# Mamba scan between two expert layers: decays two chunks ahead, two banks for the scan's outputs

## What is computed

```python
def _mamba2(u, Wi, conv_w, conv_b, dt_bias, A_log, D, norm_w, Wo):
    zxbcdt = u @ Wi.T                                    # z, xBC, dt
    xBC = silu(causal_conv4(xBC) + conv_b)               # x, B, C
    dt, A = softplus(dt + dt_bias), -exp(A_log)
    h = h * exp(dt_t * A) + (dt_t * x_t) B_t             # token by token
    y_t = h C_t + D * x_t
    y = y * silu(z)
    y = y * rsqrt(mean(y * y) + 1e-05) * norm_w
    return y @ Wo.T
x = x + 0.5 * moe(layernorm(x))
x = x + (out_f + out_b[:, ::-1]) * 0.5
x = x + 0.5 * moe(layernorm(x))
```

## Time and profile before

| what | us |
|---|---|
| median of 3 runs | 824.81 (816.74 to 825.22) |
| the profiled execution | 823.38 |
| its span in the trace | 821.5 |
| granted clock of PE, mean | 0.955 of full speed |

### The profile page before, as it was taken

One profiled execution on the slowest core, in us unless ns is written; L12 is line 12 of the kernel. 1 busy time (PEld: TensorE's weight loads), 2 busy tenths in 40 slices (PEclk: granted clock), 3 DMA queues, 4 the chain that ended last, 5 costly groups with the idle time before them and its releaser, 6 DMA issues. The chain is left out here.

```text
span 821.5 us, 13087 instructions
## 1 busy us (share of the span) xinstructions
PE 719.1 (88%) x4076; PEld 382.0 (46%) x4076; DVE 491.8 (60%) x1424; ACT 544.1 (66%) x936; POOL 278.3 (34%) x296
## 2 busy tenths in 40 slices
PE   4799999989999997898988976798897787999996
PEld 1432222212123224565655554667675675566564
DVE  6878542204865647852456659779698776533453
ACT  4367998899998993653357675884988552434441
POOL 3090003301000433434522455242443470255552
PEclk9899999999999998999989998798999899999999
DMA  4046925522492311111211032121221231222233
GB/s 135 1 180 180 191 78 95 206 75 70 175 285 79 100 38 43 35 41 52 67 55 55 20 113 66 40 64 49 73 62 40 83 96 35 65 60 58 64 100 92
DMA packets 76409, 70.10 MB, mean 85 GB/s; under 512 B 9687, under 2 KB 60233, under 8 KB 76080
## 3 DMA queue, kind: packets, MB, share of 16 engines
q1 hardware_dynamic: 71024, 60.56, 26.4%
q0 software_dynamic: 5024, 8.54, 3.2%
q10 hardware_dynamic: 288, 0.10, 0.1%
HBM read 41.23 MB, written 29.02 MB: 86 GB/s over the span
## 5 line engine op out<-in xcount | busy, mean ns | idle before, releaser
L693 ACT ACTIVATE attn_p<-attn_ps 128x1024 f32<-128x1024 f32 x256 | 241.0, 1079 | 26.0 <-PE attn_ps L686 14.6
L709 PE MATMUL attn_ps<-attn_p,attn_v 128*32 128x512 f32 x1024 | 136.4, 604 | 5.7 <-issue 5.6
L1687 PE MATMUL ps_main<-moe_xsT,moe_w 128*128 128x320 f32 x384 | 128.2, 460 | 9.1 <-issue 3.1
L1697 ACT ACTIVATE moe_act_h<-ps_main 128x320 f32<-128x320 f32 (+1 forms) x128 | 55.3, 434 | 98.3 <-PE ps_main L1687 67.4
L1712 DVE TENSOR_TENSOR moe_hid<-moe_act_h,ps_main 128x320 f32<-128x320 f32 (+1 forms) x128 | 62.0, 485 | 96.1 <-ACT moe_act_h L1697 58.0
L1580 POOL DMA_INDIRECT moe_slots<-rows,moe_scatter_at x64 | 63.6, 994 | 104.6 <-DVE moe_hid L1712 56.0
L1687 PEld LDWEIGHTS ps_main<-moe_xsT,moe_w 128*128 128x128 f32 x384 | 69.1, 196 | 42.8 <-issue 21.2
L686 PE MATMUL attn_ps<-attn_q_rows,attn_k_rows 64*128 64x512 bf16 x448 | 79.8, 385 | 6.3 <-issue 3.0
L1717 PE MATMUL ps_main<-moe_hid,moe_w 128*128 128x320 f32 (+1 forms) x256 | 75.5, 461 | 4.6 <-DVE moe_hid L1712 4.6
L686 PEld LDWEIGHTS attn_ps<-attn_q_rows,attn_k_rows 64*128 64x128 bf16 x448 | 19.0, 93 | 122.2 <-ACT attn_p L693 96.6
L2119 DVE SCALAR_TENSOR_TENSOR mb_act<-mb_padded,mb_taps,mb_act 128x1024 f32<-128x1024 f32 x48 | 67.1, 1408 | 1.3 <-ACT mb_act L2110 0.7
(11 more groups left out here) (268 smaller groups left out, 1304.3 us busy)
## 6 DMA issues: line engine op xcount, KB each, us to landing
mb_cums<-mb_cum_kept SPq DMA_DIRECT2D x32, 256.0 KB, 3.5
moe_slots<-zeros SPq DMA_DIRECT2D x4, 1380.0 KB, 13.4
attn_q_rows<-attn_q_parts SPq DMA_DIRECT2D x36, 128.0 KB
attn_k_rows<-attn_k_parts SPq DMA_DIRECT2D x36, 128.0 KB
moe_w<-in_w SPq DMA_DIRECT2D x3, 1536.0 KB, 11.3
moe_rows<-zeros SPq DMA_DIRECT2D x4, 1024.0 KB, 14.7
...
```

The source lines that it names most:

```text
L693: self.core.nc.scalar.activation(self.p[:, w % self.PB, :, :].rearrange("p a n -> p (a n)"), self.ps_s[:, w % self.SB, :, :].rearrange("p ...
L709: ins = self.core.nc.tensor.matmul(self.ps_av[32 * i:32 * i + 32, :], self.v[:, b * TPB + kt, (HGROUPS * i + m) // 2, self.window(m)], sel ...
L1687: self.core.nc.tensor.matmul(ps[:, w % 2, 0:CAP], wt[:, e, c * P:(c + 1) * P], self.xsT[:, u % 2, :], start=True, stop=True).then_inc(self ...
L1697: self.core.nc.scalar.activation(self.act_h[into, w % 2, :], self.ps_h1[rows, w % 2, 0:CAP], ACT.Silu).then_inc(self.silu_done, 1)
```

## The change

ScalarE's work for a chunk is split in three: `lower` (the four Relus), `copy_b` and `exps`. Before the loop it does lower, copy and exponential of chunk 0 and lower and exponential of chunk 1; in iteration `g` it begins with `lower(g+2)`, `copy_b(g+1)`, `exps(g+2)`. `cums` and `e_seg` get a third place, in columns of `moe.hid`, which is why SP waits for the last expert's `y_done` before the sums of chunk 2. SP's loop runs one longer, and the spread decays are issued two behind the sums.

`ps_y` has two banks and `ps_x` one. PE does `outputs(g)` right after `state(g)`, then `squares` and `output`, then the projections. The sums of squares of the last four chunks go to spare columns of `ps_st`; those of chunks 28 to 31 are formed after the loop, the last behind the last `output`.

The norm's roots move to chunk 6, its normalise for tiles 18 and 19 to chunk 6 (20 and 21 from chunk 5 to 6 of unit 2); turn, logits, routing and counts of the last expert layer each one chunk later; scatters from chunks 1 to 6 of unit 3 (3, 3, 3, 3, 3, 1) to chunks 2 to 6 (3, 3, 3, 3, 4). After the scan DVE takes the first expert's rows before the last adds, and the root search and normalise of the last tiles come between the first gatings, with turns and logits later to match. The cut diff leaves out lines that only rename a buffer's place, and lines around; its indentation is reduced.

```diff
@@ -1885,8 +1885,8 @@
-self.ps_b, self.ps_y, self.ps_st, self.ps_o = (main[:, i, :] for i in (1, 3, 4, 5))
-self.ps_x = (main[:, 0, :], main[:, 2, :])
+self.ps_x, self.ps_b, self.ps_st, self.ps_o = (main[:, i, :] for i in (0, 1, 4, 5))
+self.ps_y = (main[:, 3, :], main[:, 2, :])
@@ -1992,9 +1992,11 @@
-if g >= 2:
-    sp.wait_ge(self.lowered, g - 1)
-sp.dma_start(self.cums[:, g % 2, :, :], self.cum_dram[b, di, j].unsqueeze(0).to_broadcast([P, NH, P])).then_inc(self.cums_in[g % 2], 16)
+if g == 2:
+    sp.wait_ge(self.core.moe.y_done, B * E_)
+if g >= 3:
+    sp.wait_ge(self.lowered, g - 2)
+sp.dma_start(self.cums[g % 3], self.cum_dram[b, di, j].unsqueeze(0).to_broadcast([P, NH, P])).then_inc(self.cums_in[g % 3], 16)
@@ -2132,11 +2134,11 @@
-act, ps_x = self.act_t[:, u % 2, :, :], self.ps_x[g % 2]
+act, ps_x = self.act_t[:, u % 2, :, :], self.ps_x
...
-if g >= 2:
-    pe.wait_ge(self.x_read, g - 1)
-    pe.wait_ge(self.gm_done, g - 1)
+if g >= 1:
+    pe.wait_ge(self.x_read, g)
+    pe.wait_ge(self.gm_done, g)
@@ -2147,23 +2149,27 @@
-def exps(self, act, g):
+def lower(self, act, g):
...
-    act.wait_ge(self.cums_in[g % 2], 16 * (g // 2 + 1))
+    act.wait_ge(self.cums_in[g % 3], 16 * (g // 3 + 1))
...
-    if g >= 2:
-        act.wait_ge(self.mt_done, g - 1)
+    if g >= 3:
+        act.wait_ge(self.mt_done, g - 2)
...
-        ins = nc.scalar.activation(self.e_seg[:, g % 2, hh, :], self.cums[:, g % 2, hh, :], ACT.Relu, bias=self.cum[:, di, n, hh:hh + 1], scale=-1.0)
+        ins = nc.scalar.activation(self.e_seg[g % 3][:, hh, :], self.cums[g % 3][:, hh, :], ACT.Relu, bias=self.cum[:, di, n, hh:hh + 1], scale=-1.0)
...
+def copy_b(self, act, g):
...
-    nc.scalar.copy(self.bs[:, g % 2, :], self.ps_b[:, 0:P]).then_inc(self.b_read, 1)
+    self.core.nc.scalar.copy(self.bs[:, g % 2, :], self.ps_b[:, 0:P]).then_inc(self.b_read, 1)
...
+def exps(self, act, g):
...
-    nc.scalar.activation(self.e_seg[:, g % 2, :, :], self.e_seg[:, g % 2, :, :], ACT.Exp, scale=-1.0).then_inc(self.seg_exp, 1)
+    self.core.nc.scalar.activation(self.e_seg[g % 3], self.e_seg[g % 3], ACT.Exp, scale=-1.0).then_inc(self.seg_exp, 1)
@@ -2240,19 +2246,20 @@
-if g >= 1:
-    pe.wait_ge(self.y_read, g)
+ps_y = self.ps_y[g % 2]
+if g >= 2:
+    pe.wait_ge(self.y_read, g - 1)
@@ -2292,23 +2299,26 @@
-    if parts:
+    if u == 3 and i >= GROUP:
+        pe.wait_ge(self.h_ready, len(self.UNITS) * (self.NC - 1))
+    elif parts:
...
-    if u == 3 and i == GROUP:
-        pe.wait_ge(self.ss_read, 4)
-    col = 3 * D + n % TPB
+    at = self.sums_of(u)[:, n % TPB:n % TPB + 1] if u < 3 or i < GROUP else self.sums_of(4)[:, i:i + 1]
...
-        ins = self.core.nc.tensor.matmul(self.ps_o[:, col:col + 1], self.y2[:, g % 3, c, :], self.ones[:, 0:1], start=(c == 0), stop=(c == 1))
+        ins = self.core.nc.tensor.matmul(at, self.y2[:, g % 3, c, :], self.ones[:, 0:1], start=(c == 0), stop=(c == 1))
...
+def sums_of(self, k):
+    return self.ps_st[:, DIN:DIN + TPB] if k == 4 else self.ps_o[:, 3 * D:3 * D + TPB]
...
-    self.core.nc.vector.tensor_scalar(self.var[:, lo:hi], self.ps_o[:, 3 * D + lo:3 * D + hi], 1.0 / DIN, None, ALU.mult).then_inc(self.ss_read, 1)
+    self.core.nc.vector.tensor_scalar(self.var[:, lo:hi], self.sums_of(k)[:, lo:hi], 1.0 / DIN, None, ALU.mult).then_inc(self.ss_read, 1)
@@ -2326,7 +2336,8 @@
-pe.wait_ge(self.ss_read, self.scale_of(u, part) + 1)
+if self.scale_of(u, part) < 4:
+    pe.wait_ge(self.ss_read, self.scale_of(u, part) + 1)
@@ -2369,6 +2380,7 @@
+mamba.e_seg, mamba.cums = ([own[:, 0, :, :], own[:, 1, :, :], moe.hid[:, 1, :, i * P:(i + 1) * P]] for i, own in enumerate((mamba.e_seg, mamba.cums)))
@@ -2449,21 +2461,19 @@
-if u == 1 and i == 0:
-    pe.wait_ge(norm.ready, 20)
-if u + 1 < UNITS and i != mamba.GATES_AT:
-    for c in mamba.PIECES_AT[i]:
-        mamba.project(pe, u + 1, c)
+mamba.outputs(pe, g)
...
-if g >= 2:
+if 2 <= g <= N - 3:
...
-mamba.outputs(pe, g)
...
-if u + 1 < UNITS and i == mamba.GATES_AT:
-    mamba.project(pe, u + 1, 5)
+if u == 1 and i == 0:
+    pe.wait_ge(norm.ready, 20)
+if u + 1 < UNITS:
+    for c in mamba.PIECES_AT[i]:
+        mamba.project(pe, u + 1, c)
@@ -2471,23 +2481,24 @@
-    if u == 2 and i == 6:
+    if u == 2 and i == 7:
...
-    if u == 2 and i == 7:
+    if u == 3 and i == 0:
...
-    if u == 3 and i == 0:
+    if u == 3 and i == 1:
...
+for g in range(N - 4, N - 1):
+    mamba.squares(pe, g, 0)
+mamba.output(pe, UNITS - 1, 2)
+mamba.squares(pe, N - 1, 0)
...
-for g in (N - 2, N - 1):
-    mamba.squares(pe, g, PARTS_OUT * (UNITS - 1) + 2)
-mamba.output(pe, UNITS - 1, 2)
@@ -2509,9 +2520,11 @@
-if u == HALF and c in (1, 2):
-    norm.turn(pe, 21 + c)
-if u == HALF and c == 3:
+if u == HALF and c == 0:
+    pe.wait_ge(mamba.ss_read, len(mamba.SCALES))
+if u == HALF and c in (2, 3):
+    norm.turn(pe, 20 + c)
+if u == HALF + 1 and c == 0:
@@ -2537,13 +2550,13 @@
-for g in range(2, N + 1):
+for g in range(2, N + 2):
...
-    if g >= 3:
-        mamba.spread_decays(sp, g - 1)
+    if g >= 4:
+        mamba.spread_decays(sp, g - 2)
@@ -2576,8 +2589,8 @@
-if u == 3 and i >= 1:
-    moe.scatter(pool, 3, 3 * (i - 1), min(3 * i, TOPK * TPB))
+if u == 3 and 2 <= i <= 6:
+    moe.scatter(pool, 3, 3 * (i - 2), 3 * (i - 1) + (i == 6))
@@ -2671,8 +2684,9 @@
-if u == 0 and i in (5, 6):
-    norm.normalise(dve, ch, i + 13)
+if u == 0 and i == 6:
+    norm.normalise(dve, ch, 18)
+    norm.normalise(dve, ch, 19)
@@ -2681,20 +2695,19 @@
-    if u == 2 and i == 5:
+    if u == 2 and i == 6:
...
-    if u == 2 and i == 7:
+    if u == 3 and i == 0:
...
-    if u == 3 and i == 0:
+    if u == 3 and i == 1:
...
+moe.take(dve, HALF)
...
-moe.take(dve, HALF)
...
-norm.invert(dve, ch, 22)
@@ -2707,8 +2720,11 @@
-if u == HALF and c in (0, 1):
-    norm.normalise(dve, ch, 22 + c)
+if u == HALF and c == 0:
+    norm.invert(dve, ch, 22)
+if u == HALF and c == 1:
+    norm.normalise(dve, ch, 22)
+    norm.normalise(dve, ch, 23)
@@ -2771,13 +2787,27 @@
+mamba.lower(act, 0)
+mamba.copy_b(act, 0)
...
+mamba.lower(act, 1)
+mamba.exps(act, 1)
...
+    if g + 2 < N:
+        mamba.lower(act, g + 2)
...
-        mamba.exps(act, g + 1)
+        mamba.copy_b(act, g + 1)
+    if g + 2 < N:
+        mamba.exps(act, g + 2)
...
+    if u == 0 and i == mamba.GATES_AT:
+        norm.root(act, 18)
+        norm.root(act, 19)
+    if u == 2 and i == mamba.GATES_AT:
+        norm.root(act, 20)
+        norm.root(act, 21)
@@ -2795,9 +2825,6 @@
-if u == 0 and i == 5:
-    norm.root(act, 18)
-    norm.root(act, 19)
@@ -2805,13 +2832,10 @@
-if u == 2 and i == 5:
-    norm.root(act, 20)
-    norm.root(act, 21)
-if u == 2 and i == 6:
+if u == 2 and i == 7:
...
-if u == 2 and i == 7:
+if u == 3 and i == 0:
```

More of the change, by code:

```diff
@@ L1897, in open @@
         self.lowered = sem("lowered")
-        self.cums_in, self.e_cum_in = ([sem(f"{n}{i}") for i in range(2)] for n in ("cums_in", "e_cum_in"))
+        self.cums_in, self.e_cum_in = [sem(f"cums_in{i}") for i in range(3)], [sem(f"e_cum_in{i}") for i in range(2)]
         (self.gm_done, self.mt_done, self.xw_done, self.h_decayed, self.h_ready, self.y_read, self.gate_done) = (
@@ L2182, in front @@
                 dve.wait_ge(self.xw_done, self.passed(g - 2))
-        ps_x = self.ps_x[g % 2]
+        ps_x = self.ps_x
         nc.vector.tensor_tensor(self.by_head(self.xdt[:, g % 2, :]), self.by_head(ps_x[:, 0:DIN]), self.heads(self.dt[:, n, di * NH:(di + 1) * NH]), ALU.mult)\
@@ L2242, in outputs @@
         u, di, b, i, n, cols = self.at(g)
-        if g >= 1:
-            pe.wait_ge(self.y_read, g)
+        ps_y = self.ps_y[g % 2]
+        if g >= 2:
+            pe.wait_ge(self.y_read, g - 1)
         for c in range(2):
-            nc.tensor.matmul(self.ps_y[:, c * P:(c + 1) * P], self.skips[:, di, c * P:(c + 1) * P], self.act_t[:, u % 2, c, cols], start=(c == 0), stop=False)
+            nc.tensor.matmul(ps_y[:, c * P:(c + 1) * P], self.skips[:, di, c * P:(c + 1) * P], self.act_t[:, u % 2, c, cols], start=(c == 0), stop=False)
         if i:
@@ L2254, in outputs @@
         for hh in range(NH):
-            out = self.ps_y[HP * (hh % 2):HP * (hh % 2) + HP, hh // 2 * P:hh // 2 * P + P]
+            out = ps_y[HP * (hh % 2):HP * (hh % 2) + HP, hh // 2 * P:hh // 2 * P + P]
             ins = nc.tensor.matmul(out, self.xdt[:, g % 2, hh * HP:(hh + 1) * HP], self.mt[:, g % 2, hh, :], start=False, stop=(hh >= NH - 2))
@@ L2265, in back @@
             dve.wait_ge(self.gate_done, g - 1)
-        y_in, y_old, own = self.y_in[:, g % 2, :, :], self.y_old[:, g % 2, :, :], self.ps_y[:, 0:2 * P].rearrange("p (c t) -> p c t", c=2)
+        y_in, y_old, own = self.y_in[:, g % 2, :, :], self.y_old[:, g % 2, :, :], self.ps_y[g % 2][:, 0:2 * P].rearrange("p (c t) -> p c t", c=2)
         if i:
             dve.wait_ge(self.e_cum_in[g % 2], 32 * self.e_cums(g))
-            nc.vector.tensor_tensor(y_old, self.e_cum[:, g % 2, :, :], self.ps_y[:, 2 * P:4 * P].rearrange("p (c t) -> p c t", c=2), ALU.mult).then_inc(self.old_done, 1)
```

(5 more changed lines are left out.)

4 lines of the change are left out of this document (2 added, 2 removed).

## The result

The changed kernel takes 829.16 us (median of 8 runs, 826.04 to 832.65) against 824.97 of the kernel before beside it (8 runs, 816.74 to 828.48): 1.0062 times the time, 95% interval 1.0032 to 1.0091. The forecast was 831.0, within 1% of before. The profiled execution of the changed kernel took 829.31 us with a span of 827.5.

What follows compares the result with a forecast made beforehand. No engine was at its limit in the scan, so the chunk-to-chunk chain was taken to decide. +6.0 + 1.4 - 1.5 + 1.6 - 1.0 = +6.5 us gave 829.9, on the median's footing 831; range 820 to 838.

Steps and rivals of the forecast that it cites:

- Part 1, the start: Chunk 0 of the scan: ScalarE's Relus of chunk 2 wait for the sums' transfer, delaying take and first tap; +6.0 us.
- the lower bound of +2.1: Scan start: cost without the wait for the transfer, only from outputs(0) standing before the projection; +2.1 us.
- Rival B: Scan start: the sums' transfer lands early enough, so the start costs +2.1 and not +6.0 us; chance 0.11.
- Part 2, the boundaries: Outputs and squares before the projection on PE: +1.4 and +1.6 us at two unit boundaries, -1.5 at y(10).
- The term of y(10): Chunk 10: outputs before the projection remove y(10)'s 1.25 us wait, with 0.2 of small waits; -1.5 us.
- The two boundary terms: Chunks 8 and 16: the later projection delays the first tap and DVE's taps; +1.4 and +1.6 us.
- the sign of being wrong that I had named: First boundary: first taps of unit 2 start earlier than 12.1 us after the silu's end.
- my walk: Unit boundaries: step-by-step timing from silu through outputs, norm turn and projection to the taps; +1.4 and +1.6 us.
- Part 3, last unit and hand-over: Last unit to expert layer: last scatter +2.0, but the first expert's rows taken before the last sums; net -1.0 us.
- the sign that I had named: Last unit: the final scatter begins 2 us later relative to chunk 30's state.
- A: Unit boundaries: PE idle keeps the granted clock low, outputs and projections slow down; +4.7 us, chance 0.20.
- C: Unit boundaries: DVE counts and mask waits come off one for one; -15.1, with the start -9.1 us; chance 0.14.

Runs made afterwards that it cites:

- the first and third group: Two of three sets of follow-up runs, each on another chip; the kernel before was timed beside them at 824.71 and 824.80 us.
- tapfirst: Changed kernel, but in chunk 0 ScalarE does copy, take and first tap of unit 1 before the Relus of chunk 2; 823.35 us, 0.9971 of before.
- again_after: The changed kernel itself, unedited, once more on the third group's chip; 828.62 us against 824.80 for the kernel before.
- tap_route: Changed kernel with the first tap ahead of chunk 2's Relus, and the last layer's norm and routing back in their earlier chunks; 1.0033 of before.
- projfirst: Changed kernel with PE's projections put back ahead of the outputs in every chunk; 1.0055 of before.
- route: Changed kernel with the last expert layer's norm, routing and scatters back in the chunks of before; first expert product 215.1 us behind xdt(0).
- nolook: Changed kernel with ScalarE's decays only one chunk ahead again, buffers and PE order kept; 0.9981 of before.

## Why the prediction was right or wrong

The total came out 1.8 us below the forecast, and in the range. The steps did less well: they summed to +6.5, where the profiles show +1.4, +2.2 and +2.2 us at the first product, and +0.7, +3.1 and +1.6 from xdt(0) to the end of the span. The medians are 4.2, 6.2 and 3.8 us apart, so 2.3 to 3.5 us lie in no stage after xdt(0), and that the total came so near the forecast owes something to luck. The listed clocks give a hint: the changed kernel's runs average 0.943, 0.946 and 0.948, those of the kernel before 0.952 and 0.954 in the first and third group, and among the latter 0.01 less goes with some 5 us more. By that the lower clock would answer to some 3 us (an estimate). Whether the change lowers the clock stays open.

- **Part 1, the start: right.** Forecast +6.0, measured +6.3, +7.4 and +6.0 at y(1). Wait of 6 us forecast, 7.12 found. It decides the sign of the total: both kernels without it are at 0.9971. tapfirst, which takes the first tap out from behind the wait and keeps the outputs ahead of the projection, shows +1.7 against the lower bound of +2.1. Rival B is excluded.
- **Part 2, the boundaries: wrong, by about 5 us.** Forecast +1.5 in all, measured -4.1 from y(1) to y(17), and -3.1 in again_after. The term of y(10) was right: y(9) to y(14) has -1.9 (forecast -1.5), with y(9) to y(10) down from 7.5 to 6.2. The two boundary terms had the wrong sign: from `before(8)` to y(9) -1.3 where I had +1.4, from y(14) to y(17) -1.4 where I had +1.6. The steps that failed are `outputs(7)` at 3.1 us and the norm turn at 1.9, durations that are true of the trace of before and that I took as the operations' price.

  At the first boundary outputs(7) ran from 539.00 to 541.51, 2.5 us, and the turn took 1.07. So the projection began 7.5 us behind the silu where I had walked to 9.6, and the taps 11.3 where I had 13.4; the sign of being wrong that I had named, taps earlier than 12.1 us, came true. In again_after outputs(7) took 3.0, but the turn again 1.07, and the projection began at 7.7. The granted clock from `before(8)` to the projection was 0.81 in the changed kernel against 0.57 before.

  At the second boundary, measured from y(14) to the taps, it is 11.4 us before, and 10.4, 10.4 and 11.0 after. tapfirst and tap_route have the same order there and needed 13.9 each: in those the clock was low, and my walk, priced at that level, gives 13.1. The order was priced well for one level and the clock was at the other. From `before(16)` to the start of the projection the changed kernel and tapfirst have the same list of instructions:

```profile
590.44:595.74 5.30, 5.30 (x48) 4.62 (x49) 3.75 (x9) 5.27 (x14) 1.91 (x3) 1.00 0.03 9
```

```profile
580.52:588.90 8.38, 8.38 (x48) 7.09 (x49) 4.72 (x10) 6.92 (x18) 2.06 (x4) 0.59 0.18 47
```

  PE has no gap in either; its 48 matmuls take 5.30 us at a granted clock of 1.00, and 8.38 at 0.59. What follows, in the timeline of each, is the taps at 9.1 us behind the silu or at 12.2:

```profile
590.44 0.44 PE L2143 MATMUL ps_main<-ident,mb_act 128*128 128x128 f32 x2 [2.29 <-ACT mb_act L2128]
...
599.55 1.28 DVE L2121 SCALAR_TENSOR_TENSOR mb_act<-mb_padded,mb_taps,mb_act 128x1024 f32<-128x1024 f32 x1 [3.25 <-ACT mb_act L2112]
```

```profile
580.52 0.44 PE L2143 MATMUL ps_main<-ident,mb_act 128*128 128x128 f32 x2 [2.65 <-ACT mb_act L2128]
...
592.71 1.28 DVE L2121 SCALAR_TENSOR_TENSOR mb_act<-mb_padded,mb_taps,mb_act 128x1024 f32<-128x1024 f32 x1 [3.99 <-ACT mb_act L2112]
```

  So against the kernel before, whose own clock there was 0.72, the sign of this step goes with the clock; that the change brings the higher clock about is not shown. The mechanism of the step itself was right: DVE idles 3.42 and 3.25 us until the first tap, and the later projection costs 1.1 us at the first boundary (projfirst), where I had 1.85. In chunk 10 projfirst shows that the old order would cost 2.9.
- **Part 3, last unit and hand-over: right in sum, wrong in its parts.** Forecast -1.0; from y(17) to the product the change measures -0.8 (88.2 to 87.4). Inside, -4.4 and +3.6. I had priced the norm's roots and normalise of unit 2 at nothing; moved to chunk 6 they come off y(17) to y(22) with 2.6 us, as route shows by putting them back. I gave the last scatter +2.0 for this part, and measured from y(17) it came +1.9 (78.2 to 80.1). Its working (1.8 us saved, 3.8 lost) is not what the trace has: the sixteen scatters begin 2.5 us later and take 24.1 us instead of 24.7. From xdt(0) the last scatter is 4.0 later, 2.2 of it from the parts before; behind the state product of chunk 30, the sign that I had named, it is 3.8 later and not 2. What shortens y(25) to y(31) by 1.5 us no run isolates.
- **Rivals.** A (clock low at the boundaries) did not come in the three profiles of the changed kernel, but did at the second boundary of tapfirst and tap_route: 18.8 us from y(14) to y(17) instead of 15.3, +3.5 for one boundary where I had 4.7 for two. C (mask waits come off one for one) is excluded at the unit boundaries by nolook: 3.19 us of wait, 1.0 of time.
